# A two-layer attention and experts kernel: the last batch's key sums divided in two parts

## The chip, the core and the metric

The kernel runs on one core of a Trainium2 chip. The metric is the time of one execution on the device in microseconds, as the median of timed runs. The engines of the core are TensorE (PE in the profile), VectorE (DVE), ScalarE (ACT), GpSimd (POOL) and SyncE (SP); ScalarE and SyncE each have a queue on which they issue DMAs (ACTq, SPq).

## What is computed

Four batches of 1024 tokens with 128 features go through two layers. Layer 0 adds two branches to its input `x`: an attention with 16 heads that share one key and one value head (`_L0_attn_ref`), and a SwitchHead attention, whose values and outputs are mixed from experts (`_L0_ffn_ref`). Layer 1 adds a linear attention and a mixture of experts. The change touches the end of the first branch of layer 0:

```python
qr = q.reshape(bsz, NUM_HEADS * tgt_len, HEAD_DIM)
attn_weights = jnp.einsum('brd,bsd->brs', qr, k)
attn_probs = jax.nn.softmax(attn_weights, axis=-1)
attn_output = jnp.einsum('brs,bsd->brd', attn_probs, v)
...
out = jnp.einsum('bte,oe->bto', attn_output, Wo) + bo
x = x + out + _L0_ffn_ref(xn, ...)
```

The kernel sums the exponentials times the values (the numerators), and the exponentials alone (the denominators), over the keys, and divides afterwards.

## The kernel before, in words

**Steps.** Layer 0 runs `N0` = 32 steps: 4 batches (`B`) times 8 SwitchHead heads (`HS`). Each step does one SwitchHead head and, beside it, two of the 16 heads of the other attention, so that after the 8 steps of a batch all its heads are done. Every engine has its own written order inside `for i in range(-4, N0 + 3)`; it is a software pipeline, so that one pass of the loop holds work of several steps. The engines meet only at semaphores.

**Key sums.** In each step TensorE's `sum_by_key` (L381) accumulates numerators and denominators of two heads in the PSUM tile `sums`. ScalarE's `keep_sums` (L1031) copies them to `sumsT`, and `store_sums` (L1040) sends them with 4 DMAs to `sums_dram`, later in the pass.

**Division.** After the last step of batch b, SyncE's `load_dens` (L707) loads the denominators into `dens` (128 partitions), VectorE's `invert_dens` (L1477) inverts them, they go to `rden_dram` and are loaded again in the layout of the heads by `load_rden` (L264, 16 DMAs of 8 partitions each, into `rden_in`). The numerators are loaded by `load_o` (L719, 16 DMAs, into `o_in`). Each DMA adds 16 to `o_loaded`. POOL's `divide_o` (L806) multiplies the two, in two parts of 8 heads, and writes `oT` in the order of the tokens. For batches 0 to 2 this lies inside the steps of the next batch. For the last batch (`B - 1`) there is no next batch: SyncE does it after its loop; ScalarE sends the inverse (L1259) and loads half of it, and VectorE's `divide_last` (L1497) does the second 8 heads.

**What follows.** TensorE's `project_out` (L444) multiplies `oT` with `wo`. VectorE adds this to `x` (`add_attn`, L1506), takes the moments, normalises into `xo`, which is the same memory as `oT`; TensorE turns it (`turn_xo`, L409), ScalarE keeps the turned tiles (`keep_xoT`, L1078), SyncE stores `xo` (L729). Then the block ends, all engines meet, and layer 1 (`main1`) begins.

**What stands beside it.** At the end of the last step POOL's `sum_outputs` (L894 to L898) adds up each of eight tiles of the SwitchHead output, after VectorE's `gate_outputs` (L1362) and ScalarE's `scale_outputs` (L962) have weighted them. The buffers `oprod` are two, so tile t+2 waits for the sum of tile t. TensorE's products land in a ring of 7 PSUM tiles, each claimed anew when its earlier reader is done. Batch 2's routing comes after `keep_xoT` of batch 2: TensorE's `routing` (L454), VectorE's `keep_routing` (L1532) and `choose_experts`, ScalarE's `routing_exps` (L1121), VectorE's `mix` (L1547 to L1550). `split_layer1` (L83, L87, L1488) splits layer 1's weights in two halves each, after `mix`.

**Order after the loops.** TensorE: `routing(2)`, `project_out(3)`. ScalarE: wait for the inverse, its DMA and eight loads, `routing_exps(2)`. VectorE: `invert_dens(3)`, `keep_routing(2)`, `choose_experts(2)`, `mix(2)`, `split_layer1`, `divide_last`. POOL: `divide_o(3, 0)`. SyncE: `store_xo(2)`, `load_dens(3)`, `load_o(3)`, `store_xo(3)`.

## Time and profile before

| | |
|---|---|
| timed runs, median (lowest to highest) | 3134.33 us (3131.17 to 3143.01) |
| profiled execution, its own time | 3132.94 us |
| its span, first to last instruction | 3131.1 us |
| busy share PE / DVE / ACT / POOL | 94% / 69% / 61% / 59% |
| mean granted clock of TensorE | 0.978 of full |
| layer 0 ends, layer 1 begins | about 2588 us from the start |

The profile is of one execution. Its page gives the busy share of each engine, the span in 40 slices, the DMA queues, the chain of work that ended last and the costliest groups of instructions. From the trace one can ask for the instructions in order of time (the timeline) or for the busy time within chosen stretches. A row of the timeline has the start in us, the duration in us, the engine, the line, the operation, what is written and from what, the shape and the count; in brackets stands the idle time of the engine just before and what ended it.

### The profile page before, as it was taken

The numbers are of one execution on the slowest core, as the hardware profiler recorded it, in microseconds if no ns is written. First come the engines' busy times: TensorE is split into PE (matmuls) and PEld (weight loads), VectorE is DVE, ScalarE is ACT, GpSimd is POOL, SyncE is SP. The second block draws the span as 40 slices with busy tenths as digits, with TensorE's granted clock in tenths as the row PEclk, the third lists the DMA queues.
The fourth block names the chain that finished last, engine by engine and source line by source line (L and its number), as shares of the span: only waits on it lengthen the run. The fifth ranks groups of instructions, "written<-read, shape, count | busy, mean of one in ns | idle before, by whom it ended". The sixth has DMA issues, their size and how long they took to land. (4 is left out here: it accounts for less than half of the span.)

```text
span 3131.1 us, 53004 instructions
## 1 busy us (share of the span) xinstructions
PE 2948.8 (94%) x17486; PEld 2046.5 (65%) x17486; DVE 2145.0 (69%) x4151; ACT 1912.6 (61%) x4365; POOL 1851.9 (59%) x2333
## 2 busy tenths in 40 slices
PE   4999999999999999999999999999999967898997
PEld 2666666666666666666666666666666645566674
DVE  7777787876777877777778787777777645234343
ACT  1566666666666666667666666666666642444634
POOL 2466666676666667676766666666666544444330
PEclk7999999999999999999999999999999978999999
DMA  5000001100100011111000110010001012133222
GB/s 169 21 22 22 22 22 32 32 22 23 36 22 22 22 32 32 30 29 37 29 22 22 32 32 22 23 37 29 22 22 39 9 25 61 57 103 105 88 77 86
DMA packets 139858, 124.70 MB, mean 40 GB/s; under 512 B 28410, under 2 KB 122116, under 8 KB 139492
## 3 DMA queue, kind: packets, MB, share of 16 engines
q1 hardware_dynamic: 125892, 88.46, 10.2%
q0 software_dynamic: 10160, 30.17, 3.1%
q10 hardware_dynamic: 3536, 2.69, 0.3%
q8 instruction: 143, 2.34, 0.3%
q14 instruction: 127, 1.04, 0.1%
HBM read 97.49 MB, written 29.30 MB: 40 GB/s over the span
## 5 line engine op out<-in xcount | busy, mean ns | idle before, releaser
L1281 DVE TENSOR_REDUCE m_peaks<-m_ring 128x1 f32<-128x512 f32 x1024 | 637.0, 682 | 32.1 <-PE m_ring L293 31.5
L1022 ACT ACTIVATE m_expA<-m_ring 128x512 f32<-128x512 f32 x1024 | 545.6, 609 | 121.3 <-PE m_ring L366 113.5
L993 ACT ACTIVATE m_prob<-m_ring,m_negs 128x512 f32<-128x512 f32 x512 | 347.1, 684 | 234.8 <-DVE m_negs L1329 234.5
L884 POOL TENSOR_TENSOR m_vprod<-m_vprod 128x512 f32<-128x512 f32 x256 | 328.0, 1281 | 251.7 <-DVE m_vprod L1294 232.7
L344 PE MATMUL m_ring<-m_probT,m_vs 128*128 128x256 f32 x2048 | 471.0, 383 | 0.4 <-DVE m_peaks L1281 0.2
L894 POOL TENSOR_TENSOR m_oprod<-m_oprod 128x512 f32<-128x512 f32 x256 | 329.6, 1287 | 204.5 <-ACT m_oprod L962 202.2
L1294 DVE TENSOR_TENSOR m_vprod<-m_ring,m_gate 128x512 f32<-128x512 f32 x512 | 345.2, 688 | 126.9 <-PE m_ring L99 89.7
L344 PEld LDWEIGHTS m_ring<-m_probT,m_vs 128*128 128x128 f32 x2048 | 384.8, 190 | 69.0 <-issue 16.5
L1319 DVE TENSOR_REDUCE m_negs<-m_ring 128x1 f32<-128x512 f32 x512 | 342.5, 686 | 107.9 <-PE m_ring L99 103.5
L1003 ACT ACTIVATE m_probT<-m_ring 128x512 f32<-128x512 f32 x512 | 311.1, 617 | 98.1 <-PE m_ring L332 95.4
L962 ACT ACTIVATE m_oprod<-m_ring,m_go 128x128 f32<-128x128 f32 x1024 | 294.9, 385 | 94.4 <-PE m_ring L99 87.8
L332 PE MATMUL m_ring<-k_ident,m_prob 128*128 128x128 f32 x2048 | 309.3, 279 | 7.6 <-ACT m_prob L993 7.2
L332 PEld LDWEIGHTS m_ring<-k_ident,m_prob 128*128 128x128 f32 x2048 | 236.4, 141 | 85.0 <-issue 44.5
L381 PE MATMUL m_sums<-m_expA,m_v 128*32 128x512 f32 x2048 | 272.7, 605 | 1.4 <-ACT m_expA L1022 1.4
L1362 DVE TENSOR_TENSOR m_oprod<-m_ring,m_go 128x512 f32<-128x512 f32 x256 | 175.9, 687 | 125.9 <-PE m_ring L99 119.7
L97 PE MATMUL m_ring<-k_wvs,k_xs 128*128 128x512 f32 (+1 forms) x536 | 233.1, 435 | 18.8 <-ACT m_prob L993 14.6
L97 PE MATMUL m_ring<-m_wos,m_ctxT 128*128 128x512 f32 x512 | 223.8, 437 | 3.5 <-ACT m_expA L1022 1.7
L99 PE MATMUL m_ring<-k_wvs,k_xs 128*128 128x512 f32 (+1 forms) x536 | 211.0, 394 | 0.0
L97 PE MATMUL m_ring<-k_xs,m_yT 128*128 128x512 f32 x512 | 210.1, 410 | 0.6 <-DVE m_peaks L1281 0.2
L98 PE MATMUL m_ring<-k_wvs,k_xs 128*128 128x512 f32 (+1 forms) x536 | 209.4, 391 | 0.0
L98 PE MATMUL m_ring<-m_wos,m_ctxT 128*128 128x512 f32 x512 | 203.1, 397 | 0.0
L99 PE MATMUL m_ring<-m_wos,m_ctxT 128*128 128x512 f32 x512 | 202.5, 396 | 0.0
(317 smaller groups left out, 5481.6 us busy)
## 6 DMA issues: line engine op xcount, KB each, us to landing
m_wraw<-in_v_w SPq DMA_DIRECT2D x32, 512.0 KB, 4.2
m_qf<-q_dram SPq DMA_DIRECT2D x128, 128.0 KB, 2.6
m_wraw<-in_o_w SPq DMA_DIRECT2D x32, 512.0 KB, 4.2
q_dram<-m_kf SPq DMA_DIRECT2D x24, 256.0 KB, 4.6
listed<-in_pad SPq DMA_DIRECT2D x6, 897.0 KB, 11.5
m_xg<-listed SPq DMA_DIRECT2D x39, 138.0 KB, 2.2
m_rows<-answers SPq DMA_DIRECT2D x8, 512.0 KB, 4.3
sums_dram<-m_sumsT ACTq DMA_DIRECT2D x128, 18.0 KB
```

The costliest lines, as they stand in the source:

```text
L97: pe.matmul(out, wh, xh, start=True, stop=False)
L98: pe.matmul(out, wh, xl, start=False, stop=False)
L99: return pe.matmul(out, wl, xh, start=False, stop=True)
L332: last = pe.transpose(ps[:, c * P:(c + 1) * P], prob[t % 2][:, (4 * h + c) * P:(4 * h + c + 1) * P], ident[:, :])
L344: last = pe.matmul(ps[:, 0:2 * P], vs[n % 2][:, k, :], probT[g % 2][:, k, :], start=(k == 0), stop=(k == TPB - 1))
L884: vchain(pool.tensor_tensor(vprod[:, 0:512], vprod[:, 0:512], vprod[:, 512:1024], ALU.add))
L894: ochain(pool.tensor_tensor(op[:, 0:512], op[:, 0:512], op[:, 512:1024], ALU.add))
L993: act.activation(prob[t % 2][:, c * 512:(c + 1) * 512], ring.home["scores", n, t, c][:, :], ACT.Exp, bias=neg[t % 2], accum_out=den[n % 2] ...
L1022: act.activation(expA[hh][:, c * 512:(c + 1) * 512], ring.home["scT", n, k, hh, c][:, :], ACT.Exp)\
L1281: v.tensor_reduce(peaks[:, t, hh, c:c + 1], ring.home["peaks", n, t, hh, c][:, :], AX.X, ALU.max)\
L1294: v.tensor_tensor(vprod[:, c * 512:(c + 1) * 512].rearrange("p (e d) -> p e d", e=4), ring.home["values", n, t, c][:, :].rearrange("p (e d ...
L1319: v.tensor_reduce(half_neg[:, t % 2, c:c + 1], ring.home["scores", n, t, c][:, :], AX.X, ALU.max, negate=True)\
```

## The change

The key sums of the last batch are treated in two parts: `early`, heads 0 to 11 (steps 24 to 29), and `late`, heads 12 to 15 (steps 30 and 31).

- ScalarE sends the sums of the last step right behind their copy, not at the end of the pass.
- SyncE, after its loop, first loads the denominators of the early heads (96 partitions) and their numerators, waits for the inverse, sends it to DRAM and loads it again; then comes the store of batch 2's tiles; then the late heads: 16 DMAs that spread the denominators straight from `sums_dram`, and 16 for the numerators. ScalarE's part of these DMAs is gone.
- VectorE inverts the early denominators inside the last step (ahead of `gate_outputs(31, 0)`); POOL divides the early heads in `o_in` inside the last step, between `sum_outputs(31, 1)` and `sum_outputs(31, 2)`; ScalarE copies them to `oT` after its loop.
- VectorE, after `mix(2)`, inverts the late denominators in place (4 heads x 64 on 128 partitions) and divides the late heads into `oT`.
- `split_layer1` moves from the end of VectorE's queue to the last step, ahead of `gate_outputs(31, 4)`.
- `project_out` of the last batch waits for one more count of `o_divided`.

```diff
-                    pe.wait_ge(o_divided, 2 * (b + 1))
+                    pe.wait_ge(o_divided, 2 * (b + 1) + (b == B - 1))
...
+                early, late = slice(0, 12), slice(12, H0)
+                closing = sums_dram[(B - 1) % 2].rearrange("h (i c) k (g u) -> c g k (h i) u", i=2, g=HD)
+
+                def load_heads(heads):
+                    for c in range(2):
+                        for g in range(HD):
+                            rows = slice(64 * c + HD * g, 64 * c + HD * (g + 1))
+                            sp.dma_start(o_in[rows, heads, :], closing[c, g, 0:HD, heads, :]).then_inc(o_loaded, 16)
+
+                def load_early_heads():
+                    sp.wait_ge(sums_stored, 64 * (N0 - 2))
+                    sp.wait_ge(rden_stored, 16 * (B - 1))
+                    sp.wait_ge(o_divided, 2 * (B - 1))
+                    sp.dma_start(dens[0:96, :], sums_dram[(B - 1) % 2][0:6, :, HD, :].rearrange("h j (s r) -> (h j) s r", s=4))\
+                        .then_inc(dens_loaded, 16)
+                    load_heads(early)
+                    sp.wait_ge(dens_inverted, B)
+                    sp.dma_start(rden_dram[(B - 1) % 2][0:24].rearrange("g (s r) -> g s r", s=4), dens[0:96, :]).then_inc(rden_stored, 16)
+                    sp.wait_ge(rden_stored, 16 * B)
+                    rden_of = rden_dram[(B - 1) % 2].rearrange("(h c) (g u) -> c g h u", c=2, g=HD)
+                    for c in range(2):
+                        for g in range(HD):
+                            rows = slice(64 * c + HD * g, 64 * c + HD * (g + 1))
+                            sp.dma_start(rden_in[rows, early, :], rden_of[c, g, early, :].partition_broadcast(HD)).then_inc(o_loaded, 16)
+
+                def load_late_heads():
+                    sp.wait_ge(sums_stored, 64 * N0)
+                    sp.wait_ge(o_divided, 2 * B - 1)
+                    for c in range(2):
+                        for g in range(HD):
+                            rows = slice(64 * c + HD * g, 64 * c + HD * (g + 1))
+                            sp.dma_start(rden_in[rows, late, :], closing[c, g, HD, late, :].partition_broadcast(HD)).then_inc(o_loaded, 16)
+                    load_heads(late)
...
+                load_early_heads()
                 store_xo(B - 2)
-                load_dens(B - 1)
-                load_o(B - 1)
+                load_late_heads()
                 store_xo(B - 1)
...
+                def divide_early_heads():
+                    pool.wait_ge(o_loaded, 512 * B)
+                    pool.tensor_tensor(o_in[:, 0:12, :], o_in[:, 0:12, :], rden_in[:, 0:12, :], ALU.mult).then_inc(o_divided, 1)
...
                     sum_values(i + 3, 7)
+                    if i == N0 - 1 - 2:
+                        divide_early_heads()
                     sum_outputs(i + 2, 2)
...
-                divide_o(B - 1, 0)
...
                     act.activation(sumsT[:, :], sums[:, :], ACT.Copy).then_inc(sums_kept, 1)
+                    if n == N0 - 1:
+                        send_sums(n)
+
+                def place_early_heads():
+                    act.wait_ge(o_divided, 2 * B - 1)
+                    act.wait_ge(xo_turned, 2 * (B - 1))
+                    act.wait_ge(xo_stored, 16 * FILLS + 16 * (B - 1))
+                    act.activation(oT[:, :].rearrange("p (u h) -> p h u", h=H0)[:, 0:12, :], o_in[:, 0:12, :], ACT.Copy)\
+                        .then_inc(o_divided, 1)
...
-                act.wait_ge(dens_inverted, B)
-                act.dma_start(rden_dram[(B - 1) % 2].rearrange("g (s r) -> g s r", s=4), dens[:, :]).then_inc(rden_stored, 16)
-                load_rden(act, B - 1, (1,))
+                place_early_heads()
                 routing_exps(B - 2)
...
+                def invert_early_heads():
+                    v.wait_ge(dens_loaded, 16 * B)
+                    v.reciprocal(dens[0:96, :], dens[0:96, :]).then_inc(dens_inverted, 1)
+
+                def divide_late_heads():
+                    v.wait_ge(o_loaded, 512 * (B + 1))
+                    v.reciprocal(rden_in[:, 12:H0, :], rden_in[:, 12:H0, :]).then_inc(dens_inverted, 1)
+                    v.wait_ge(dens_inverted, B + 1)
                     v.wait_ge(xo_turned, 2 * (B - 1))
                     v.wait_ge(xo_stored, 16 * FILLS + 16 * (B - 1))
-                    heads = slice(8, 16)
...
+                    v.tensor_tensor(oT[:, :].rearrange("p (u h) -> p h u", h=H0)[:, 12:H0, :], o_in[:, 12:H0, :],
+                                    rden_in[:, 12:H0, :], ALU.mult).then_inc(o_divided, 1)
...
                     output_gates(i, 3)
+                    if i == N0 - 1:
+                        split_layer1()
                     gate_outputs(i, 4)
...
                     gate_values(i + 2, 5, 0)
+                    if i == N0 - 1 - 1:
+                        invert_early_heads()
                     gate_outputs(i + 1, 0)
...
-                invert_dens(B - 1)
                 keep_routing(B - 2)
                 choose_experts(B - 2)
                 mix(B - 2)
-                split_layer1()
-                divide_last()
+                divide_late_heads()
```

## Rows read from the trace of the kernel before

**Rows 1.** Busy time by stretch: us, engines (instructions), PEclk, DMA share, GB/s
```profile
2558.00:2576.00 18.00, 0.03 (x1) 0.00 (x0) 6.87 (x24) 1.54 (x2) 1.99 (x1) 0.50 0.59 53
2588.00:2700.00 112.00, 91.33 (x754) 66.78 (x755) 43.41 (x96) 44.08 (x53) 59.72 (x63) 0.94 0.18 53
```

**Rows 2.** Timeline of TensorE, 2547 to 2580 us
```profile
2554.45 3.58 PE L454 MATMUL m_ring<-m_gw,k_xnT 128*128 128x8 f32 x16 [7.14 <-ACT k_xnT L1078]
2576.07 3.78 PE L444 MATMUL m_ring<-m_wo,m_oT 128*128 128x128 f32 x16 [18.04 <-POOL m_oT L806]
```

**Rows 3.** Timeline of ScalarE and its DMA queue, 2540 to 2565 us
```profile
2540.71 0.60 ACT L1031 ACTIVATE m_sumsT<-m_sums 128x512 f32<-128x512 f32 x1 [0.67 <-PE m_sums L381]
2543.77 2.18 ACT L962 ACTIVATE m_oprod<-m_ring,m_go 128x128 f32<-128x128 f32 x8 [2.47 <-DVE m_go L1344]
...
2551.43 0.37 ACT L962 ACTIVATE m_oprod<-m_ring,m_go 128x128 f32<-128x128 f32 x1 [1.79 <-POOL k_x L898]
2551.54 0.27 ACTq L1040 DMA_DIRECT2D sums_dram<-m_sumsT  x1
...
2553.31 1.08 ACT L1078 ACTIVATE k_xnT<-m_ring 128x512 f32<-128x512 f32 x2 [0.73 <-issue]
...
2564.36 0.26 ACT L1121 ACTIVATE m_lg<-m_lg 128x64 f32<-128x64 f32 x1 [9.97 <-issue]
```

**Rows 4.** Timeline of SyncE's DMA queue, 2554 to 2565 us
```profile
2554.40 0.56 SPq L707 DMA_DIRECT2D m_dens<-sums_dram  x1
2555.01 5.98 SPq L719 DMA_DIRECT2D m_o_in<-sums_dram  x16
2561.33 2.96 SPq L264 DMA_DIRECT2D m_rden_in<-rden_dram  x8
```

**Rows 5.** Timeline of VectorE, 2544 to 2575 us
```profile
2544.30 1.29 DVE L1362 TENSOR_TENSOR m_oprod<-m_ring,m_go 128x512 f32<-128x512 f32 x2
...
2556.49 0.95 DVE L1477 RECIPROCAL m_dens<-m_dens 128x128 f32<-128x128 f32 x1 [3.07 <-DMA m_dens<-sums_dram]
2558.07 0.23 DVE L1532 TENSOR_TENSOR m_lg<-m_ring,m_gb 128x64 f32<-128x64 f32 x1 [0.62 <-PE m_ring L454]
...
2561.42 0.23 DVE L1541 TENSOR_TENSOR m_lg<-m_lg,m_t_first 128x64 f32<-128x64 f32 x1
2564.65 0.23 DVE L1547 TENSOR_TENSOR m_lg<-m_lg,m_t_sel 128x64 f32<-128x64 f32 x1 [3.01 <-ACT m_lg L1121]
...
2565.55 0.69 DVE L83 CAST k_wvs<-k_spare 128x384 fp32r<-128x384 f32 x2
...
2567.35 0.16 DVE L1488 TENSOR_SCALAR k_spare<-k_spare 128x2 f32<-128x2 f32 x1
2573.97 1.02 DVE L1497 TENSOR_TENSOR m_oT<-m_o_in,m_rden_in 128x512 f32<-128x512 f32 x1 [6.45 <-DMA m_rden_in<-rden_dram]
```

**Rows 6.** Timeline of POOL, 2536 to 2576 us
```profile
2536.54 1.27 POOL L894 TENSOR_TENSOR m_oprod<-m_oprod 128x512 f32<-128x512 f32 x1 [3.35 <-ACT m_oprod L962]
...
2545.07 1.30 POOL L894 TENSOR_TENSOR m_oprod<-m_oprod 128x512 f32<-128x512 f32 x1 [2.27 <-DVE m_oprod L1362]
...
2574.01 2.00 POOL L806 TENSOR_TENSOR m_oT<-m_o_in,m_rden_in 128x512 f32<-128x512 f32 x1 [16.51 <-DMA m_rden_in<-rden_dram]
```

**Rows 7.** Timeline of ScalarE's DMA queue: the sums of step 29
```profile
2450.16 1.37 ACTq L1040 DMA_DIRECT2D sums_dram<-m_sumsT  x4
```

**Rows 8.** Timeline of all engines in the last step, 2521 to 2524 us
```profile
2521.27 0.69 DVE L1362 TENSOR_TENSOR m_oprod<-m_ring,m_go 128x512 f32<-128x512 f32 x1
...
2523.60 0.66 PE L332 MATMUL m_ring<-k_ident,m_prob 128*128 128x128 f32 x4
```

**Rows 9.** Groups of VectorE by form: line, count, busy us, mean ns
```profile
L2364 DVE RECIPROCAL m_oden<-m_oden 128x512 f32<-128x512 f32 x8 | 26.8, 3353 | 0.3
```

**Rows 10.** Timeline of SyncE's DMA queue, batch 2's division
```profile
2072.89 0.35 SPq L722 DMA_DIRECT2D rden_dram<-m_dens  x1
2075.80 6.32 SPq L264 DMA_DIRECT2D m_rden_in<-rden_dram  x16
```

More of the change, by code:

```diff
@@ L255, in layer0, with load_rden @@
         steps, batches = range(N0), range(B)
-        def load_rden(eng, b, parts):
+        def load_rden(eng, b):
             eng.wait_ge(rden_stored, 16 * (b + 1))
             rden_of = rden_dram[b % 2].rearrange("(h c) (g u) -> c g h u", c=2, g=HD)
-            for c in parts:
+            for c in range(2):
                 for g in range(HD):
@@ L719, in load_o @@
                             sp.dma_start(o_in[rows, :, :], sums_of[c, g, 0:HD, :, :]).then_inc(o_loaded, 16)
-                    if b < B - 1:
-                        sp.wait_ge(dens_inverted, b + 1)
-                        sp.dma_start(rden_dram[b % 2].rearrange("g (s r) -> g s r", s=4), dens[:, :]).then_inc(rden_stored, 16)
-                    load_rden(sp, b, range(2) if b < B - 1 else (0,))
+                    sp.wait_ge(dens_inverted, b + 1)
+                    sp.dma_start(rden_dram[b % 2].rearrange("g (s r) -> g s r", s=4), dens[:, :]).then_inc(rden_stored, 16)
@@ new lines, in load_o @@
+                    load_rden(sp, b)
+                early, late = slice(0, 12), slice(12, H0)
[5 more added lines that the diff above has]
+                            sp.dma_start(o_in[rows, heads, :], closing[c, g, 0:HD, heads, :]).then_inc(o_loaded, 16)
@@ L725, in store_xo @@
+                def load_late_heads():
+                    sp.wait_ge(sums_stored, 64 * N0)
+                    sp.wait_ge(o_divided, 2 * B - 1)
+                    for c in range(2):
+                        for g in range(HD):
+                            rows = slice(64 * c + HD * g, 64 * c + HD * (g + 1))
+                            sp.dma_start(rden_in[rows, late, :], closing[c, g, HD, late, :].partition_broadcast(HD)).then_inc(o_loaded, 16)
+                    load_heads(late)
                 def store_xo(b):
@@ L1031, in keep_sums, with send_sums @@
                     act.activation(sumsT[:, :], sums[:, :], ACT.Copy).then_inc(sums_kept, 1)
+                    if n == N0 - 1:
[6 more added lines that the diff above has]
+                        .then_inc(o_divided, 1)
                 def store_sums(n):
-                    if n not in steps:
-                        return
+                    if n in range(N0 - 1):
+                        send_sums(n)
+                def send_sums(n):
                     act.wait_ge(sums_kept, n + 1)
@@ L1488, in split_layer1 @@
                     v.tensor_scalar(w["bqk"], w["bqk"], DN, None, ALU.mult)
-                def divide_last():
-                    v.wait_ge(o_loaded, 512 * B)
-                    v.wait_ge(out_made, 2 * (B - 1))
+                def invert_early_heads():
[5 more added lines that the diff above has]
+                    v.wait_ge(dens_inverted, B + 1)
                     v.wait_ge(xo_turned, 2 * (B - 1))
                     v.wait_ge(xo_stored, 16 * FILLS + 16 * (B - 1))
-                    heads = slice(8, 16)
-                    v.tensor_tensor(oT[:, :].rearrange("p (u h) -> p h u", h=H0)[:, heads, :], o_in[:, heads, :],
-                                    rden_in[:, heads, :], ALU.mult).then_inc(o_divided, 1)
+                    v.tensor_tensor(oT[:, :].rearrange("p (u h) -> p h u", h=H0)[:, 12:H0, :], o_in[:, 12:H0, :],
+                                    rden_in[:, 12:H0, :], ALU.mult).then_inc(o_divided, 1)
                 def add_attn(b, q):
```

## Prediction

> **What bounds the kernel now.** The page first: its busy shares name TensorE as the engine that sets the pace, and its slices show that share holding near nine tenths except in a few slices four fifths of the way along. That is where layer 0 ends, and it is the only place that the diff touches. I then read the stretches around it, and the timeline of each engine there. In 2558 to 2576 us TensorE does 0.03 us of work in 18 while the DMA engines are busy 0.59 of the time [rows 1]. TensorE's own row says what ends the pause: `project_out` of the last batch starts at 2576.07 after 18.04 us idle, released by the division on POOL [rows 2]. What has to be read next is each engine's order of work from the last key sums (2541) to that start. ScalarE copies the sums at 2540.71, but starts sending them only at 2551.54, behind all four of its remaining scalings [rows 3]. SyncE then loads the denominators (2554.40), the sums (16 DMAs from 2555.01) and, after the inverse has gone to DRAM and back, the inverse (from 2561.33, half on ScalarE's queue) [rows 4]. VectorE and POOL start dividing at 2573.97, released by that load [rows 5, 6]. So the pause is a round trip through DRAM that begins 10 us late. Everything after it is a chain of engines that begins with `project_out`; a start earlier by g ends the kernel earlier by g unless something named below takes it back.
>
> **Sending the last sums at once.** `keep_sums` ends at 2541.31 (2540.71 + 0.60). Four sends take 1.37 us in an undisturbed step [rows 7], so ScalarE is free at 2542.7; its next work began at 2543.77 after waiting for VectorE's gates [rows 3], so this costs nothing. Should that cover go, it is 1.4 us. From the first send to SyncE's next load went 2554.40 - 2551.54 = 2.86 us [rows 3, 4], so the late loads can start at 2544.2.
>
> **The early heads, in the last step.** SyncE is past its last weight load by then; the needed sums are sent at 2450.16 [rows 7], 70 us before VectorE gets to `invert_early_heads`. That stands just ahead of the gate multiply at 2521.27 [rows 8]. Its price is that of the 128x128 inverse, 0.95 us [rows 5], the free size being the same with 96 partitions. The multiply behind it then ends at 2522.9 in place of 2521.96; the next taker of its PSUM buffer, seven claims on, is the transpose at 2523.60 [rows 8]. So nothing, at worst the 0.95. Then: store and reload 2.91 us (2072.89 to 2075.80 in batch 2 [rows 10]; 3.9 by the last batch), 16 loads 6.32 us [rows 10], to 2531.4; landing 2.1 us after the issue as for the denominators (2554.40 to the inverse at 2556.49 [rows 4, 5]), or 9.7 us as in the tail of before (issue ends 2564.29, division starts 2573.97 [rows 4, 5]). I take the first, because there one queue loads while others rest, as in batch 2: 2533.5; the high end is 2541.1. `divide_early_heads` on POOL, 768 elements a lane, is 1.5 times the 1.27 us of an addition of 512, 1.9 us (high end 1.5 x 2.00, the last batch's division, 3.0) [rows 6]. Queued behind the waiting instruction are six `sum_outputs`, first of them at 2536.54 [rows 6]; for them wait the gate multiplies and scalings of tiles 4 to 7. Ending at 2535.4 it costs nothing. At the high end (2544.1) it pushes that row by 7.6 us; the pause of 2.27 us ahead of 2545.07 [rows 6], and the 1.96 us of the next paragraph, leave 3.3 us of loss. SyncE's store of batch 2's tiles waits behind these loads, but its input is only ready at about that time, and its taker is the write to `oT` 20 us later. The ScalarE copy of 12 heads (1.5 x 0.60 = 0.9 us by [rows 3]) stands in a wait of ScalarE for VectorE's routing.
>
> **`split_layer1` moved up.** It takes 2567.51 - 2565.55 = 1.96 us [rows 5]. It leaves the end of VectorE's queue and comes ahead of the gate multiply at 2544.30 [rows 5]. POOL's sum of tile 4 (2545.07) was waiting for exactly that multiply, so it starts at 2547.03. ScalarE's last scaling starts 6.36 us after that sum (2551.43 - 2545.07 [rows 3, 6]): now 2553.4. Four scalings are 1.1 us (half of the x8 row), the two copies of `keep_xoT` 1.08 us, with no sends between: they end at 2555.6 in place of 2554.39. The move is paid back entirely later, so by itself it is worth nought; but it decides when the routing starts. POOL's last sum ends some 2 us later too, at 2559.5, well before anything needs it.
>
> **What is late next.** Between ScalarE's copies and the last division stands batch 2's routing, which before was hidden under the DMAs and now is the path. From TensorE's row to VectorE's (2554.45 to 2558.07) 3.62 us [rows 2, 5]; choosing to 2561.65, 3.58 us; the exponential, which before was stuck behind ScalarE's eight loads until 2564.36 [rows 3] and now follows at once, 0.32 us; mixing, 2564.65 to 2565.55, 0.90 us [rows 5]. Sum 8.42: from 2555.65 to 2564.07. Then the new inverse of four heads, 256 elements: between 0.95 for 128 [rows 5] and 3.35 for 512 [rows 9], on that line 1.75 us; the division of 256, half of 1.02 [rows 5], 0.51 us; hand-overs 0.1 us. `project_out` starts at 2566.4.
>
> **The late loads** must have landed by 2564.07. They are 32 DMAs, only a quarter as long each but by the rows the issue sets their pace: 32 x 6.32 / 16 = 12.6 us, from 2544.2 to 2556.8 (12.0 with the 5.98 of [rows 4]). Landing 2.1 us later is 2558.9, hidden by 5 us; landing 9.7 us later is 2566.5, which shows 2.4 us. I take the low end, since they carry a quarter of the last batch's packets on a single queue.
>
> **The sum.** 2576.07 - 2566.4 = 9.7 us, against a span of 3131.1 and a profiled time of 3132.94: 3123.2. The median of the three timed runs is 1.4 us above that execution; by it the changed kernel is at 3124.6. I say 3124.
>
> **Rivals.** (1) *The late loads bind*: the 9.7 us landing comes back, because packets this small drain slowly. For it: the DMA share of 0.59 in [rows 1] with the issue long over. Against it: 1024 packets of 256 B, not 4096. The gain is 7.3 us, 3126. (2) *The early loads hold POOL*, the one that ends slower: the loads stand at the head of POOL's queue in front of six sums that all the rest waits for. They cost nothing if landed by about 2537.9 (2536.54 + 2.27 + 1.96, less 1.9 for the division, is 2538.9, less hand-overs and a margin of 1). From there each us costs one; at 2548.5 the gain is gone; at 2564 the loss is 15.7. With a landing at 2560 the time is 3135, at 2568 it is 3143. The slow tail reaches only 2541 (3127), so a loss needs a delay that no row shows. (3) *TensorE's clock*. It is at 0.50, that is 1.2 GHz, through the pause [rows 1], and the 112 us from 2588 have a mean of 0.94: 13.4 us at the lower level, worth at most 6.7 us. TensorE's pause ahead of the routing was 7.14 us [rows 2]; now its last transposes wait for the buffer of tile 4's multiply, up to 2549, and 6.6 us are left. That is little less, so I expect it to fall again; but if it stays at 2.4 GHz, or comes back at once, the time is 3117 to 3120. The Trainium skill, in "TensorE: Matmul & The Clock Gate", Part 1, says that the check of activity runs freely and isn't tied to the kernel's work; by that rule a shift of 10 us alone can move both edges, either way. (4) *The change gives nothing*: a wait after `project_out` that I take to be a consequence is tied to something fixed, 3133. I find no such thing: all engines meet at the end of the block, 12 us on.
>
> **How the numbers follow.** Forecast 0.62 (own range 3120 to 3129); late loads 0.14 (3126); clock 0.10 (3118); nothing gained 0.08 (3133); POOL held 0.06 (3127 to 3143). The range, 3117 to 3133, takes in the clock and the high ends of both loads, and leaves out the bad half of (2). 0.5% of the median is 15.7 us, about what a measurement of this kernel can tell from no change. The sum is 9.7, so the forecast, (1) and (4) lie within it; over it goes the best part of (3), under it the worst part of (2): faster 0.08, same 0.88, slower 0.04.
>
> **What would show it.** In the changed kernel: sends right behind the copy at about 2541.3; SyncE's 32 late loads from 2544; early division on POOL before 2536 and the first sum behind it not moved; sum of tile 4 at 2547; routing on TensorE at 2555.6; VectorE going from mixing straight into the inverse with no idle for a DMA; `project_out` at 2566.4. The prediction is wrong if VectorE idles before that inverse for `rden_in` or `o_in`, if POOL idles past 2537 for them, if the last step's TensorE pauses grow, or if the distance from `project_out` to the end, 555 us, changes by more than 2 us.

## The result, and the profile after

The changed kernel takes 3127.44 us, median of 10 executions (3119.89 to 3129.39); the kernel before, on the same chip, 3135.15 (10 executions, 3127.54 to 3143.01). The ratio is 0.997, interval 0.9957 to 0.9982: faster by 0.3%, less than the 0.5% named in the prediction, and 3.4 us above the forecast of 3124 (3117 to 3133). The means differ by 9.3 us, with a standard error of 1.8 (3135.8 - 3126.4). The profiled execution took 3129.17 us, with a span of 3127.2. Two executions far above all others are left out of every comparison below: one of the kernel before on the chip called C there (12688 us) and one of the early inverse three times on the same chip (3705 us, at a granted clock of 0.74).

The four fences below are timelines of the changed kernel, one engine each, from the last key sums to the start of layer 1: start us, duration us, engine, line, operation, and in brackets the idle time ahead of it with what ended it. TensorE first; its rows answer to [rows 2].

```profile
2539.29 1.06 PE L381 MATMUL m_sums<-m_expA,m_v 128*32 128x512 f32 x8
...
2546.72 0.47 PE L97 MATMUL m_ring<-m_wos,m_ctxT 128*128 128x512 f32 x1 [1.26 <-DVE m_oprod L1409]
...
2555.18 3.59 PE L454 MATMUL m_ring<-m_gw,k_xnT 128*128 128x8 f32 x16 [6.64 <-ACT k_xnT L1127]
2566.02 3.78 PE L444 MATMUL m_ring<-m_wo,m_oT 128*128 128x128 f32 x16 [7.25 <-DVE m_oT L1547]
...
2577.91 3.56 PE L2116 MATMUL m_ring<-k_spare,k_xnT 128*128 128x8 f32 x16 [0.94 <-PEq L266]
```

`project_out` (L444) starts at 2566.02 in place of 2576.07, and waits 7.25 us in place of 18.04, now for VectorE. The row at 2546.72 is a pause that the kernel before doesn't have: the last SwitchHead products wait for the multiply of tile 4, which now stands behind `split_layer1`. The last row is the first one of layer 1 (2587.97 before). ScalarE and its queue, then SyncE's queue, to be held against [rows 3, 4, 10]:

```profile
2540.45 0.60 ACT L1069 ACTIVATE m_sumsT<-m_sums 128x512 f32<-128x512 f32 x1 [0.67 <-PE m_sums L381]
2541.08 1.37 ACTq L1089 DMA_DIRECT2D sums_dram<-m_sumsT  x4
2543.52 2.18 ACT L1000 ACTIVATE m_oprod<-m_ring,m_go 128x128 f32<-128x128 f32 x8 [2.47 <-DVE m_go L1391]
...
2554.03 1.10 ACT L1127 ACTIVATE k_xnT<-m_ring 128x512 f32<-128x512 f32 x2
2554.98 1.55 ACT L1077 ACTIVATE m_oT<-m_o_in 128x768 f32<-128x768 f32 x1
```

```profile
2521.94 0.32 SPq L741 DMA_DIRECT2D rden_dram<-m_dens  x1
2523.47 7.05 SPq L747 DMA_DIRECT2D m_rden_in<-rden_dram  x16
...
2543.64 5.43 SPq L755 DMA_DIRECT2D m_rden_in<-sums_dram  x16
2549.11 6.21 SPq L731 DMA_DIRECT2D m_o_in<-sums_dram  x16
```

The four sends stand right behind the copy and leave the next scaling's start where it was (2543.52, after the same wait of 2.47 us). The late loads begin 2.56 us after the first send. POOL, to be held against [rows 6]:

```profile
2532.89 1.86 POOL L844 TENSOR_TENSOR m_o_in<-m_o_in,m_rden_in 128x768 f32<-128x768 f32 x1
2536.27 1.27 POOL L931 TENSOR_TENSOR m_oprod<-m_oprod 128x512 f32<-128x512 f32 x1 [1.53 <-ACT m_oprod L1000]
...
2546.66 1.28 POOL L931 TENSOR_TENSOR m_oprod<-m_oprod 128x512 f32<-128x512 f32 x1 [4.11 <-DVE m_oprod L1409]
```

The early division carries no bracket: it waited for nothing. The sum behind it starts at 2536.27, before 2536.54. VectorE, to be held against [rows 5]:

```profile
2558.80 0.23 DVE L1582 TENSOR_TENSOR m_lg<-m_ring,m_gb 128x64 f32<-128x64 f32 x1 [3.80 <-PE m_ring L454]
...
2562.70 0.23 DVE L1597 TENSOR_TENSOR m_lg<-m_lg,m_t_sel 128x64 f32<-128x64 f32 x1 [0.32 <-ACT m_lg L1170]
...
2563.59 1.75 DVE L1543 RECIPROCAL m_rden_in<-m_rden_in 128x256 f32<-128x256 f32 x1
2565.37 0.59 DVE L1547 TENSOR_TENSOR m_oT<-m_o_in,m_rden_in 128x256 f32<-128x256 f32 x1
```

From routing to `project_out` there is no idle time for a DMA any more. Up to the start of layer 1 the profile thus shows 10.06 us gained (2587.97 - 2577.91), 0.26 of it already there at the last sums. But the span is only 3.9 us shorter. The other 6.2 us went in layer 1. The windows of both kernels, 0 to 100, 100 to 250, 250 to 400 us and the rest from the start of layer 1 (busy us of PE, PEld, DVE, ACT and POOL, then the granted clock, DMA share and GB/s); before:

```profile
2587.97:2687.97 100.00, 83.24 (x693) 62.57 (x697) 42.66 (x94) 35.32 (x42) 51.98 (x55) 0.93 0.18 53
2687.97:2837.97 150.00, 129.64 (x1075) 91.50 (x1068) 56.30 (x113) 71.84 (x100) 60.16 (x62) 0.94 0.28 86
2837.97:2987.97 150.00, 137.87 (x1164) 103.03 (x1162) 62.54 (x144) 75.46 (x120) 57.49 (x58) 0.99 0.34 101
2987.97:3131.10 143.13, 121.32 (x1027) 89.64 (x1025) 57.91 (x104) 52.40 (x81) 28.93 (x28) 0.95 0.26 79
sum 543.13, PE 472.06 PEld 346.73 DVE 219.41 ACT 235.03 POOL 198.56; mean PE 118.02 PEld 86.68 DVE 54.85 ACT 58.76 POOL 49.64
```

and changed:

```profile
2577.91:2677.91 100.00, 83.19 (x701) 62.57 (x705) 43.77 (x94) 35.33 (x42) 52.37 (x55) 0.93 0.18 53
2677.91:2827.91 150.00, 130.20 (x1049) 90.06 (x1037) 55.75 (x106) 70.41 (x99) 59.19 (x61) 0.91 0.29 85
2827.91:2977.91 150.00, 138.78 (x1164) 104.25 (x1165) 61.38 (x145) 74.32 (x117) 56.77 (x57) 0.98 0.33 97
2977.91:3127.20 149.29, 126.39 (x1046) 94.03 (x1044) 61.30 (x112) 54.97 (x86) 30.35 (x30) 0.94 0.26 81
sum 549.29, PE 478.56 PEld 350.91 DVE 222.19 ACT 235.03 POOL 198.68; mean PE 119.64 PEld 87.73 DVE 55.55 ACT 58.76 POOL 49.67
```

Layer 1 is 6.2 us longer, TensorE is busy in it 6.5 us longer, and from 100 us on its clock is lower (0.91 against 0.94, 0.98 against 0.99, 0.94 against 0.95). The matmuls are the same, and the length of each window times its granted clock adds up to 518 us before and 517 changed, an estimate from these rounded clocks: the lower clock accounts for the length. Whether an earlier start of layer 1 costs this each time, or one execution happened to have it, is the main question that the two profiles leave. The others: which part of the change bought the 10 us, and how near each cover was to its end.

### The profile page after: what moved, and what is told of

It reads as the page before. It is cut to its first block and busy times, and to the rows that moved or that the text cites. A ratio compares the mean times of both kernels' runs of the same rounds, so it can differ in the third digit from the quotient of the medians.

```text
span 3127.2 us, 53037 instructions
## 1 busy us (share of the span) xinstructions
PE 2955.4 (95%) x17486; PEld 2050.4 (66%) x17486; DVE 2148.8 (69%) x4152; ACT 1914.0 (61%) x4366; POOL 1855.2 (59%) x2333
```

## The experiments

The runs went to three chips; the two rows without a letter are the pair of the result, timed together on one chip. Times are compared only with those of the kernel before on the same chip: mean 3173.5 us on chip A (7 executions), 3134.2 on chip B (25), 3178.3 on chip C (28). Distances are from the start of the last key sums in each kernel's own profile, because that start itself varies (2536.0 to 2539.7).

| kernel (chip) | to `project_out` | to layer 1 | layer 1 to end | mean time less before's |
|---|---|---|---|---|
| before (profile shown) | 36.5 | 48.4 | 543.1 | |
| changed (profile shown) | 26.7 | 38.6 | 549.3 | -9.3 ± 1.8 |
| sends alone (A) | 26.4 | 38.3 | 578.1 | -15.9 ± 1.9 |
| split back (A) | 26.8 | 38.7 | 576.7 | one execution |
| late numerators twice (A) | 26.7 | 38.6 | 581.3 | one execution |
| early inverse twice (A) | 28.8 | 40.7 | 577.9 | one execution |
| early inverse three times (B) | 35.1 | 47.0 | 549.3 | one execution |
| late division first (B) | 20.4 | 33.4 | 552.4 | -11.2 ± 1.4 |
| filled pauses (B) | 25.7 | 36.2 | 546.0 | -9.1 ± 1.5 |
| both (B) | 21.6 | 33.2 | 547.6 | -11.2 ± 1.4 |
| changed (C) | 26.7 | 38.6 | 589.5 | -9.9 ± 1.1 |
| sends alone (C) | 26.8 | 38.7 | 590.2 | -9.6 ± 1.0 |
| late division first (C) | 19.8 | 32.8 | 592.5 | -15.1 ± 1.3 |
| early inverse three times (C) | 34.9 | 46.8 | 590.1 | -0.1 ± 1.1 |

The errors are standard errors, from the scatter of the executions.

### The sends alone

The kernel before, with nothing changed but the place of the last step's sends.

```diff
                     act.activation(sumsT[:, :], sums[:, :], ACT.Copy).then_inc(sums_kept, 1)
+                    if n == N0 - 1:
+                        send_sums(n)
 
                 def store_sums(n):
-                    if n not in steps:
-                        return
+                    if n in range(N0 - 1):
+                        send_sums(n)
+
+                def send_sums(n):
```

> The kernel before, with one part of the change alone: the last step's sums are sent right behind their copy (2541.3 instead of 2551.5). Everything else stays: all 16 heads divided at the end, inverse through DRAM and back, half its loads on ScalarE's queue. Theory A (the 9.7 us between the last inverse load's issue and the division were the draining of the numerators that were still queued ahead): the numerators go out 10 us earlier and have landed; VectorE can invert only at 2553.4 behind its gate multiplies, the inverse loads are issued by 2561.2 and land soon after, VectorE's own queue (choice, mixing, split) is then the path, and project_out starts at 2566 to 2567, 9 us earlier, nearly all that the whole change brings. Theory B (those 9.7 us were the inverse loads' own draining, 2048 small packets from two queues at 61 GB/s): they land at about 2568 to 2570 and project_out starts at 2570 to 2572, 4 to 6 us earlier.

Measured: 3157.35 us against 3175.69, ratio 0.9949 (0.9932 to 0.9966). `project_out` starts 26.4 us after the last sums, which is 2566.0 on the clock of before, as theory A has it: all that the whole change gains in layer 0. The chain from the inverse on, from the timelines of VectorE, the two DMA queues, POOL and TensorE:

```profile
2551.25 0.94 DVE L1481 RECIPROCAL m_dens<-m_dens 128x128 f32<-128x128 f32 x1
...
2553.79 2.83 SPq L264 DMA_DIRECT2D m_rden_in<-rden_dram  x8
2553.80 2.98 ACTq L264 DMA_DIRECT2D m_rden_in<-rden_dram  x8
...
2561.77 2.06 POOL L806 TENSOR_TENSOR m_oT<-m_o_in,m_rden_in 128x512 f32<-128x512 f32 x1 [6.36 <-DMA m_rden_in<-rden_dram]
2561.78 1.02 DVE L1501 TENSOR_TENSOR m_oT<-m_o_in,m_rden_in 128x512 f32<-128x512 f32 x1
...
2563.88 3.78 PE L444 MATMUL m_ring<-m_wo,m_oT 128*128 128x128 f32 x16 [8.79 <-POOL m_oT L806]
```

The inverse loads land 5.0 us after their issue (2556.78 to 2561.77). VectorE reaches its half of the division at that very time, with its routing and `split_layer1` done and no wait. So the DRAM round trip, once it begins with the sends, takes as long as VectorE's own queue. TensorE is released by POOL's half, which also starts with the landing and ends 1.03 us after VectorE's. The division in two parts removes the round trip and POOL's half, but puts an inverse of 1.75 us on VectorE's queue behind the routing; that queue then sets the start, and nothing is gained.

### `split_layer1` back behind the mixing

```diff
                     output_gates(i, 3)
-                    if i == N0 - 1:
-                        split_layer1()
                     gate_outputs(i, 4)
...
                 mix(B - 2)
+                split_layer1()
                 divide_late_heads()
```

> The changed kernel with split_layer1 put back behind mix(2). Theory A (the routing of batch 2 is the path and the move is a nil trade): ScalarE's copies end 2.0 us earlier (2553.2 instead of 2555.1), the routing starts at 2553.2, mixing ends at 2561.8, the split takes 1.96 us, project_out starts at 2566.0 plus or minus 0.3, as in the changed kernel. Theory B (the late loads are the path): project_out stays at 2566.0 as well, but VectorE idles for the DMA in front of the inverse; if the move alone brought the gain, project_out comes at 2568.

Measured: 3156.56 us in one execution; `project_out` 26.8 us after the last sums against 26.7. TensorE's routing starts at 2553.26 in place of 2555.18: it starts earlier by what the division is then late. The move is worth nothing, as its two sides in the prediction said.

### The late numerators loaded twice

```diff
                     load_heads(late)
+                    sp.wait_ge(o_loaded, 512 * (B + 1))
+                    load_heads(late)
...
-                    v.wait_ge(o_loaded, 512 * (B + 1))
+                    v.wait_ge(o_loaded, 512 * (B + 1) + 256)
```

> The changed kernel with the 16 late numerator loads issued a second time after the first have landed, which adds 16 DMAs (6.2 us of issue) and a landing to the late loads. Theory A (they had 6 us to spare): landed at 2565.7 instead of 2557.4, project_out 2 us later than 2566.0, at 2568. Theory B (the late loads end last): project_out 8 us later, at 2574.

Measured: 3158.31 us in one execution, and no cost in layer 0: 26.7 us, where theory A expected 2 us more. Timelines of SyncE's queue and VectorE:

```profile
2546.38 13.01 SPq L731 DMA_DIRECT2D m_o_in<-sums_dram  x32
...
2560.84 1.75 DVE L1545 RECIPROCAL m_rden_in<-m_rden_in 128x256 f32<-128x256 f32 x1
```

The second copy's issue ends at 2559.39, and the inverse starts at 2560.84 without a wait: the landing took 1.45 us at most. The late loads of the changed kernel (issued until 2555.32, needed at 2563.59) have over 6 us to spare; the rival in which they bind was far away.

### The early inverse loaded twice, and three times

The 16 early loads are repeated, each round behind the landing of the last; same data, a later division on POOL.

```diff
-                    for c in range(2):
-                        for g in range(HD):
+                    for again in range(2):
+                        sp.wait_ge(o_loaded, 512 * B - 256 + 256 * again)
+                        for c in range(2):
+                            for g in range(HD):
...
-                    pool.wait_ge(o_loaded, 512 * B)
+                    pool.wait_ge(o_loaded, 512 * B + 256)
```

> The changed kernel with the 16 early inverse loads issued twice, the second time after the first have landed: POOL's early division comes at about 2541.5 instead of 2532.9. Theory A (POOL's queue has 5.5 us of cover: 1.5 us of idle ahead of the sum of tile 2 and 4.1 ahead of that of tile 4): the sum of tile 2 moves by 7.2 us, that of tile 4 by 3, project_out by 3 us, to 2569. Rival (the early division is free wherever it lies, because POOL's sums aren't the path): project_out stays at 2566. Rival (no cover): project_out moves by 8.6 us, to 2574.6.

> The changed kernel with the 16 early inverse loads issued three times, each after the last have landed: POOL's early division at about 2550.5. Theory A (5.5 us of cover, then 1:1): the sum of tile 4 moves by 12 us, project_out to about 2578, later than before the change (2576.07). Rival (POOL's sums aren't the path): 2566.

Timeline of POOL, the division held back; twice:

```profile
2539.13 1.84 POOL L846 TENSOR_TENSOR m_o_in<-m_o_in,m_rden_in 128x768 f32<-128x768 f32 x1 [7.01 <-DMA m_rden_in<-rden_dram]
2540.92 1.29 POOL L933 TENSOR_TENSOR m_oprod<-m_oprod 128x512 f32<-128x512 f32 x1
...
2544.41 1.71 POOL L933 TENSOR_TENSOR m_oprod<-m_oprod 128x512 f32<-128x512 f32 x1
```

and three times, with a row of TensorE's timeline:

```profile
2545.57 1.80 POOL L846 TENSOR_TENSOR m_o_in<-m_o_in,m_rden_in 128x768 f32<-128x768 f32 x1 [14.25 <-DMA m_rden_in<-rden_dram]
2547.33 1.26 POOL L933 TENSOR_TENSOR m_oprod<-m_oprod 128x512 f32<-128x512 f32 x1
...
2572.84 3.78 PE L444 MATMUL m_ring<-m_wo,m_oT 128*128 128x128 f32 x16 [7.26 <-DVE m_oT L1549]
```

Measured: 3158.88 us and 3135.77 us, one execution each, on two chips. Twice costs 2.1 us in layer 0 (28.8 against 26.7; 3 expected), three times 8.4 (35.1; 12 expected). The expectations counted the total cover about right (5.5 us; the division came 7.1 and 14.3 us later, which leaves 5.0 and 5.9) but had the repeated loads land too late: on the changed kernel's clock the division came at 2539.9 and 2547.1, not at 2541.5 and 2550.5.

With three rounds the first sum behind the division is pushed by 12.6 us (2547.33, against 2536.27 less the 1.57 us by which this execution is ahead) and `project_out` by 8.4: the queue holds 4.2 us of cover, beyond which each us costs one. With two rounds the first sum is pushed by 5.5 us (2540.92, 0.81 us ahead), which leaves 1.2 to pay; the other 0.8 went into POOL's first two sums, which took 3.49 and 3.55 us from start to start in place of 3.10, while VectorE did `split_layer1` beside them. Of the 10 us gained, 1.4 are left with three rounds (35.1 against 36.5).

### The late division ahead of the routing

With the loads landed, the next limit is VectorE's order: it does batch 2's routing, which only the next layer needs, ahead of the division for which TensorE waits. Here the division stands first.

```diff
+                divide_late_heads()
                 keep_routing(B - 2)
                 choose_experts(B - 2)
-                mix(B - 2)
-                divide_late_heads()
...
                     normalise_out(B - 1, q, 1)
+                mix(B - 2)
```

> The changed kernel with VectorE's order behind its loop turned: divide_late_heads first, then keep_routing and choose_experts of batch 2, and mix(2) last, behind normalise_out. Theory A (the late heads have landed at about 2557.4 and only the routing holds the division up): inverse from 2557.4, project_out at 2559.9, 6 us earlier than in the changed kernel; VectorE then chooses experts until 2563.5 while TensorE projects, so add_attn starts at 2563.5 instead of 2568.1 and the rest of the kernel 4.6 us earlier than in the changed kernel, 13 to 14 us earlier than before (ratio to before about 0.9955). Theory B (late loads or a barrier hold it up): less than 1 us.

Measured: 3122.25 us against 3132.85, ratio 0.9964 (0.9952 to 0.9977). Timelines of TensorE and VectorE:

```profile
2557.49 3.78 PE L444 MATMUL m_ring<-m_wo,m_oT 128*128 128x128 f32 x16 [0.91 <-DVE m_oT L1547]
```

```profile
2555.06 1.75 DVE L1543 RECIPROCAL m_rden_in<-m_rden_in 128x256 f32<-128x256 f32 x1 [2.24 <-DMA m_o_in<-sums_dram]
2556.85 0.59 DVE L1547 TENSOR_TENSOR m_oT<-m_o_in,m_rden_in 128x256 f32<-128x256 f32 x1
```

TensorE's pause ahead of `project_out` is down from 7.25 us to 0.91, its start 6.3 us earlier (20.4 against 26.7), the start of layer 1 5.2 (33.4 against 38.6), since batch 2's choice of experts now stands between the division and `add_attn` on VectorE. The late loads bind for the first time, by 2.24 us. They landed 1.39 us after their issue (until 2553.67). Theory A gave the starts to within 0.6 us; its 13 to 14 us of time were 11.2 on this chip and 15.1 on chip C, below.

### Filled pauses

Matmuls whose result nobody reads keep TensorE going through the pauses; they are extra work and change no output.

```diff
+                def fill(n):
+                    pe.wait_ge(sums_kept, N0)
+                    for k in range(n):
+                        pe.matmul(sums[:, :], yT[:, 0, 0:P].bitcast(F32R), xs[1][:, 0, 0:512].bitcast(F32R),
+                                  start=True, stop=True)
+
+                fill(24)
                 routing(B - 2)
+                fill(26)
                 project_out(B - 1, 0)
                 project_out(B - 1, 1)
+                fill(22)
                 turn_xo(B - 1, 0)
```

> The changed kernel with TensorE kept busy in its three last pauses of layer 0: 24, 26 and 22 matrix multiplications of 512 columns with operands already there, written over the finished tile of key sums, whose result nobody reads; the output is unchanged. They are sized to end before the work they wait for. If the granted clock stays at 2.4 GHz through the pauses: routing 1.8 us shorter, project_out's first half 1 us, the turns 0.8, the start of layer 1 about 3.4 us, so the start of project_out at 2564.2 and the whole 7 us shorter than the changed kernel, and layer 1 starts at the full clock. If the clock isn't held by this work: no change, or slower by what the fillers overrun.

Measured: 3124.61 us against 3132.85, ratio 0.9974 (0.9962 to 0.9986). The window of 2545 to 2575 us, first of this kernel, then of the changed one (columns as above):

```profile
2545.00:2575.00 30.00, 26.76 (x139) 21.59 (x137) 17.98 (x65) 7.73 (x17) 10.92 (x16) 0.94 0.09 27
```

```profile
2545.00:2575.00 30.00, 9.82 (x46) 8.60 (x46) 17.18 (x58) 7.25 (x18) 11.48 (x16) 0.59 0.04 9
```

At a clock of 0.94 in place of 0.59 the routing takes 1.95 us in place of 3.59 and `project_out` 2.05 in place of 3.78. Layer 1 starts 2.4 us earlier (36.2 against 38.6). No gain in time over the changed kernel is seen, where 7 us were expected: each is set against before on its own chip, and 9.1 ± 1.5 stands beside 9.3 ± 1.8, so that even the 2.4 us can't be told from nothing. In layer 1 the clock is hardly better for the fillers: 0.95, 0.94, 0.98 and 0.94 in the four windows, against 0.93, 0.91, 0.98 and 0.94.

The same with the division first, with 24, 11 and 32 of these matmuls:

> Both: VectorE divides first and TensorE is kept busy in the pauses (24, 11 and 32 matrix multiplications; the output is unchanged). If the two gains add: project_out at 2560, add_attn at about 2562 to 2563, layer 1 from 2572, the whole 10 to 12 us shorter than the changed kernel, ratio to before about 0.9935. If the lengths of layer 1 vary between executions by some us whatever happens in layer 0, the distance from project_out to the end scatters by 3 to 6 us beyond that in every one of these runs.

Measured: 3123.74 us, ratio 0.9961 (0.9949 to 0.9973), mean 3123.0, the same as without them (3123.0). `project_out` stands at 21.6 us in place of 20.4, behind the 11 extra matmuls, and layer 1 starts at 33.2 in place of 33.4: they take back nearly all that the clock gives.

### Four kernels on one chip, to size layer 1

On chip B the three faster kernels gained 12 to 15 us up to layer 1 and only 9.1 to 11.2 in all; in the changed kernel's own profile 9.8 came ahead of layer 1 and the span was 3.9 shorter. Either layer 1 gives back part of any earlier start, or this is scatter. For scatter speaks the early inverse three times on chip B: it starts layer 1 only 1.4 us earlier than before, and its profile still has a layer 1 of 549.3 us. Four kernels whose layer 0 differs by 14 us went to one chip, each timed:

> The changed kernel itself once more, on the same chip as the three next to it. In layer 0 its project_out stands 26.7 us behind the start of the last key sums (before: 36.5), so if layer 1 is the same length on the average, it is 9.8 us shorter than before; if part of the gain is given back in layer 1, whatever starts earlier, less: about 6 to 8 us. Its own profile should show again 26.7 us, and a layer 1 that differs by some us from that of the first profile.

> The kernel before with the early sending alone. Its first profile put project_out 26.4 us behind the last key sums, 0.3 us earlier than in the changed kernel. If that holds, its time is that of the changed kernel within 1.5 us on the same chip, and the division in two parts adds nothing by itself. Rival: the two-part division has a value that the first comparison, made on another chip, hid; then the changed kernel is 4 us or more faster than this one.

> The changed kernel with VectorE dividing the late heads ahead of batch 2's routing. Layer 1 started 5.2 us earlier than in the changed kernel, counted from the last key sums (33.4 against 38.6). If layer 1 is the same length on the average, it is 5 us shorter than the changed kernel; if the gain is given back in layer 1, 0 to 3 us.

> The changed kernel with the early inverse loads issued three times: layer 1 starts 8.4 us later, counted from the last key sums (47.0 against 38.6), 1.4 us before that of the kernel before (48.4). If layer 1 doesn't depend on when it starts, the time is 8.4 us above the changed kernel and 1.4 below before. If a layer 1 that starts later is shorter, as the medians of the first runs hint, it is only 4 to 6 us above the changed kernel.

Measured medians: changed 3168.46, sends alone 3169.42, division first 3162.01, inverse three times 3178.88, before 3179.29; ratios 0.997 (0.9961 to 0.9979), 0.9974 (0.9965 to 0.9983), 0.9958 (0.9945 to 0.9971), 1.0003 (0.9994 to 1.0013). The gains by means, 9.9, 9.6, 15.1 and 0.1 us, stand beside gains up to layer 1 of 9.8, 9.7, 15.6 and 1.6 (48.4, from the profile shown of before, less each distance; before has no profile on this chip). Every one is within 1.5 us. Without before, between the two ends of the row, 14.0 us of layer 0 are 15.0 of time, error 1.6. On this chip no give-back is seen, with errors of 1.0 to 1.6 us. The kernel with three rounds is 9.8 us above the changed one, where 8.4 were expected without a give-back and 4 to 6 with one. The changed kernel and the sends alone are the same within 0.3 us, error 1.2. The sends alone on this chip show the same tie as on chip A, now with a wait of VectorE for the load:

```profile
2563.96 1.02 DVE L1501 TENSOR_TENSOR m_oT<-m_o_in,m_rden_in 128x512 f32<-128x512 f32 x1 [0.28 <-DMA m_rden_in<-rden_dram]
```

## Why the prediction was right, and where it was not

**The number.** The sum of 9.7 us is the gain of layer 0 (9.8) and the gain of the means (9.3 ± 1.8). By the medians it is 7.7.

**The sends, and the late loads' start** were right: free of cost, and SyncE starts 2.56 us after the first send (2.86 forecast), at 2543.64 (2544.2).

**The early chain** was right in its conclusion and loose in its terms. The inverse went at 2520.97; the gate multiply behind it ended at 2522.45 in place of 2521.96, and TensorE did the same 40.14 us of work between 2500 and 2541. Store and reload took 1.53 us (2521.94 to 2523.47) where 2.91 were taken from batch 2, the 16 loads 7.05 where 6.32 were. Their landing is not seen directly, since POOL didn't wait; in the two kernels that repeat them it took 1.74 us (2543.83 to 2545.57, 2537.39 to 2539.13). The high end of 9.7 us did not come back in any of these loads. Two of these misses, the faster store and the slower issue, cancel within 0.7 us, which is luck; the cover would have hidden either. POOL's division took 1.86 us (1.9) and ended at 2534.75 (2535.4).

**POOL held.** The rival's law held: the cover is 4.2 us, which is the 2.27 + 1.96 of its working; the point from which it decides is 2539.0 on the clock of before (division at 2545.57, plus 1.83 us between the two profiles' last sums, less the 8.4 lost), where the working had 2538.9 and then took off 1 us of margin, not needed. In the changed kernel's own profile the point is 0.26 us earlier, 2538.7, and the division started at 2532.89, 5.8 us ahead of it. The law doesn't cover the 0.8 us that the sums lose beside VectorE's `split_layer1` with two rounds. The rival's times for late landings are also added up wrong: with the gain gone at 2548.5, a landing at 2560 gives about 3146 us and one at 2568 about 3154 by the same law, not 3135 and 3143. No run went that far.

**`split_layer1`** was a nil trade, as forecast, shown by undoing it. It does open the pause of 1.26 us at 2546.72, so the sign "the last step's TensorE pauses grow" came true just behind the last sums, by the wait that rival (3) of the prediction foresaw; the pause ahead of the routing is shorter by 0.5 us (6.64, forecast 6.6), and the clock fell as expected, to 0.50 from 2553 to 2566. POOL's sum of tile 4 started at 2546.66 (2547.03), the copies ended at 2555.13 (2555.6).

**The routing chain** came to 8.41 us from TensorE's row to the inverse (2555.18 to 2563.59; 8.42). Then 1.75 for the inverse (1.75) and 0.59 for the division (0.51). ScalarE's copy of 12 heads took 1.55 us where 0.9 was scaled from a contiguous copy of the same engine; it ended at 2556.53, long before anyone needed it. `project_out` started at 2566.02, against 2566.4; less the 0.26 us by which the last sums were early, 9.8 us gained against 9.7.

**The landing** was the term most overrated. The 9.7 us of the old tail [rows 4, 5] were 5.0 and 5.4 with the sends alone, and 1.45 or less on the single queue of the changed kernel. A likely cause, only argued: in the kernel before the inverse loads are issued straight behind 16 loads of numerators, and with the sends alone the numerators had been issued 5 us earlier. The DMA share between the last issue and the landing hardly tells the two apart, 0.62 and 0.52. Whatever the cause, the long landing went with the late start. The overrating cost the forecast nothing, since every landing was hidden.

**What was credited with the gain.** The sum is right but its attribution is too wide. The prediction takes round trip and late start as one and lets the whole change remove them. The step that failed to be asked is: what is late next after the sends alone? The rows of before hint at it: the old chain, moved up whole by the 10.46 us between the old and the new send (2551.54 to 2541.08), has `project_out` at 2565.6, ahead of the 2566.4 of the forecast. It does not move whole. With the sends alone VectorE's inverse comes only 3.1 us earlier (13.8 us after the last sums in place of 16.9), behind its gate multiplies; the reload then follows 2.3 us sooner and lands 4.7 us sooner, 10.1 in all. So the diff's larger part, the early heads, could bring nothing while VectorE's routing stood ahead of the division. With VectorE's order changed as well it pays, by 5.2 us. The sends alone with that order were not run; there TensorE's release waits for the landing at 2561.77, not for the routing, so that the order by itself should bring nothing: this is argued.

**The distance from `project_out` to the end** was to stay within 2 us of 555, and the single profile shows 561.2. By the prediction's own test that was a failure, and the lower clock goes with it: TensorE's busy time in layer 1 grew by 6.5 us at the same work. On chip C, by means over 5 to 28 executions, no dependence of layer 1 on its start is seen: a measured 9.9 us for 9.8. So the test was too tight for one execution; no term of layer 0 accounts for the 3.4 us between forecast and median either. The scatter is larger than the bound of 2 us: over 25 executions of the kernel before on chip B the standard deviation is 5.0 us, and the time falls by 2.3 us for each 0.001 of mean granted clock (correlation -0.85). Where the scatter lies can't be read from these times; between the profiles even the start of the last sums varies by 3.7 us. The clock rival, as an effect of the change, is not borne out in the means. The Trainium skill, "TensorE: Matmul & The Clock Gate", Part 1, has the check of activity run on its own time, not the kernel's; the mean clock's variation from 0.973 to 0.979 over those 25 executions of one kernel agrees with that, but no run here tests the rule.

What stays open: on chip B the reordered and the filled kernels gained 3 to 4 us less in the mean than up to layer 1 (standard error 1.4), and on chip A the sends alone gained 15.9, where 10 are seen in layer 0 (error 1.9); the three single executions there are 14.6 to 16.9 below before, where 8 to 10 are seen. Both are two to three standard errors and of opposite signs; within a chip all comparisons share one mean of before, so they are not independent. Chip-dependent effects of the start of layer 1 are not ruled out.

**The version that beats both** is the one with the late division first: 0.9964 and 0.9958 of the kernel before on two chips, and 5.2 us (error 1.5) below the changed kernel on chip C.

## What to carry to other kernels

When an engine pauses for a chain through DRAM, first find when the chain begins; an early start alone may bring it level with the next limit, and a costlier removal of the chain then gains nothing until that limit, here the order of VectorE's queue, is moved too. A landing time read from one tail is no property of the transfer (here 9.7, 5.0 and 1.7 us for loads of the inverse): price it as an upper bound, and look at what was issued ahead of it. And a difference of a few us in the rest of one profiled execution is no evidence of a give-back, until the means of several executions on one chip show it.

## What was not expected of the hardware

- The kernel before takes 39 to 44 us longer on chips A and C than on B. In the profiles of one kernel on two chips layer 0 ends within 2.2 us of itself, and the difference is in layer 1: 549.3 us for the changed kernel in the result's profile, 589.5 on chip C. POOL's 64 sends of rows by lists stand there. The first starts at 2611.9 and 2612.0, the last at 2720.8 and 2755.6: 34.7 of the 40 us, with each send taking 0.96 us in both. What holds them up on chip C was not tried.
- VectorE's CAST of 128x384, 0.69 us in the changed kernel, took 1.23 us where the delayed POOL queue put POOL's sums beside it (early inverse twice, at 2542.17; both figures are for a row of two). POOL's addition of 128x512 at 2544.41, beside it, took 1.71 us in place of 1.28.
- The issue of 16 DMAs takes 5.4 to 7.1 us on SyncE: 5.43 us for 4 heads of denominators, 6.21 for 4 heads of numerators, 5.98 for all 16 heads of numerators [rows 4], 7.05 for 12 heads of inverse. The count set the pace, hardly the bytes.
- Extra matmuls hold TensorE's clock at 0.94 through 30 us that else have 0.59, and make the routing's matmuls 1.8 times as fast; in the mean time of the kernel no gain is seen (9.1 us against 9.3 below before, error 2.3).
